# Four layers in one launch: other steps for two expert products of the last loop, and another order of tangents, weights and products

## What is computed

```python
# last attention: 16 heads of width 8, scores + a band mask, softmax, product with values, output matrix
x = x + L3_xattn(layernorm(x), ctx, ...)
# last feed-forward
y = layernorm(x)
logits = einsum('bsd,ed->bse', y, gate_w)               # 8 per token
topk_vals, topk_idx = top_k(logits, 2)
w = softmax(topk_vals)                                   # the two weights: (1 - t)/2, (1 + t)/2 with t = tanh(gap / 2)
full = scatter of w to 8 columns (six zeros)
expert_out = einsum('bsd,edh->bseh', y, weight)         # all eight experts
x = x + einsum('bse,bseh->bsh', full, expert_out)
```

## Time and profile before

| | |
|---|---|
| three runs | 846.9, 847.32, 849.75 us; median 847.32 us |
| profiled execution | 847.17 us |
| its span | 845.1 us (2.07 us lie around it) |
| last loop's steps 20 to 33, to the last store's issue | 805.4 to 841.5 us of the span |
| instructions | 20299 |

### The profile page before, as it was taken

One profiled execution on the slowest core, in us unless ns is written; L12 is line 12 of the kernel. 1 busy time (PEld: TensorE's weight loads), 2 busy tenths in 40 slices (PEclk: granted clock), 3 DMA queues, 4 the chain that ended last, 5 costly groups with the idle time before them and its releaser, 6 DMA issues.

```text
span 845.1 us, 20299 instructions
## 1 busy us (share of the span) xinstructions
PE 807.0 (95%) x7358; PEld 565.4 (67%) x7358; DVE 634.4 (75%) x1586; ACT 563.0 (67%) x1598; POOL 286.8 (34%) x587
## 2 busy tenths in 40 slices
PE   8999999999999999899999999999999989899986
PEld 8887888899998987554444444444466665676652
DVE  5678777777777665766966967756999967899876
ACT  3666667777767776686455666465577779888654
POOL 4246444455444335200000000002156630435445
PEclk9999999999999999999999999999999999999999
DMA  8700000000000000000000000000000000000000
GB/s 337 170 2 1 1 1 2 1 2 1 1 2 2 2 1 2 1 0 1 1 0 1 1 1 0 1 0 1 1 28 4 3 3 1 3 3 3 2 28 26
DMA packets 7886, 13.54 MB, mean 16 GB/s; under 512 B 4342, under 2 KB 5100, under 8 KB 7532
## 3 DMA queue, kind: packets, MB, share of 16 engines
q1 hardware_dynamic: 7788, 12.24, 4.6%
HBM read 11.19 MB, written 1.05 MB: 14 GB/s over the span
## 4 chain that ended last, share of the span: by engine, by line
PE 68%; DVE 14%; ACT 8%; issue 5%; POOL 4%; DMA 1%; DVEq 0%; POOLq 0%; SPq 0%; ACTq 0%
PE psum L1561 10%; PE psum L772 7%; PE psum L812 6%; PE psum L840 6%; PE psum L755 5%; PE psum L764 3%; ACT arena L910 2%; PE psum L1547 2%; PE psum L1570 2%; PE psum L2016 2%; PE psum L790 2%; PE psum L2401 2%; PE psum L829 2%; PE psum L2523 2%; PE psum L1986 2%
## 5 line engine op out<-in xcount | busy, mean ns | idle before, releaser
L517 POOL TENSOR_TENSOR ve<-mv,epsv 128x1 f32<-128x1 f32 x176 | 35.7, 203 | 422.0 <-DVE mv L512 422.0
L1561 PE MATMUL psum<-arena,w1f 128*128 128x512 f32 x240 | 109.5, 592 | 0.0
L520 POOL TENSOR_TENSOR rstd<-ve,epsv 128x1 f32<-128x1 f32 x176 | 101.3, 575 | 13.8
L910 ACT ACTIVATE arena<-psum,negmax 128x128 f32<-128x128 f32 x256 | 90.3, 405 | 22.2 <-DVE negmax L1010 22.2
L1561 PEld LDWEIGHTS psum<-arena,w1f 128*128 128x128 f32 x240 | 45.5, 190 | 48.6 <-issue 44.3
L1100 POOL TENSOR_TENSOR arena<-arena,rsum 128x512 f32<-128x512 f32 x64 | 65.7, 1046 | 24.6 <-DVE rsum L1016 24.6
L1010 DVE TENSOR_REDUCE negmax<-psum 128x8 f32<-128x1024 f32 x32 | 39.2, 1225 | 32.9 <-PE psum L812 32.9
L910 ACT ACTIVATION_READ_ACCUMULATOR arena<-psum,negmax 128x1 f32 x256 | 63.0, 246 | 0.0
L526 DVE TENSOR_SCALAR yln<-x_tok,mv,rstd 128x128 f32<-128x128 f32 x128 | 56.7, 454 | 7.9 <-POOL rstd L520 7.5
L755 PE MATMUL psum<-arena,sclA 128*128 128x128 f32 x512 | 62.5, 275 | 0.1
L772 PE MATMUL psum<-arena 128*128 128x512 f32 x128 | 61.5, 599 | 0.9 <-DVE arena L1005 0.6
(11 more groups left out here) (375 smaller groups left out, 1968.3 us busy)
## 6 DMA issues: line engine op xcount, KB each, us to landing
w<-in_w0qk SPq DMA_DIRECT2D x2, 512.0 KB, 4.9
w<-in_w0vo SPq DMA_DIRECT2D x1, 1024.0 KB, 7.6
cT<-in_cT SPq DMA_DIRECT2D x1, 1024.0 KB, 14.7
out<-x_tok SPq DMA_DIRECT2D x4, 256.0 KB, 2.2
rows<-in_rows SPq DMA_DIRECT2D x1, 836.0 KB, 12.3
x_tok<-in_x_tok SPq DMA_DIRECT2D x1, 768.0 KB, 9.7
ctx_tok<-in_ctx_tok SPq DMA_DIRECT2D x1, 768.0 KB, 10.9
wa<-in_wa SPq DMA_DIRECT2D x1, 768.0 KB, 16.8
```

The lines of the kernel that those rows point to most:

```text
L520: pool.tensor_tensor(rstd[:, u, self.i:self.i + 1], ve[:, u, self.i:self.i + 1], epsv[:, 1:2], ALU.pow) \
L910: m = nc.scalar.activation(e0[:, b, g, :], ps(k, P, j * P), ACT.Exp, bias=negmax0[:, b, g:g + 1], accum_out=sum0[:, b, g:g + 1])
L1561: nc.tensor.matmul(ps(k), w1("e2", j * 384 + arg * D, j * 384 + (arg + 1) * D), f1_Hm[:, n, 2 * j + i, :], start=False, stop=False)
```

## The change

It edits one table and two lists. Nothing else is touched, and no instruction is added or removed. Tile 6's products go from step 21 to step 20, tile 8's from step 23 to step 22. On ACT the tangent of a group stands ahead of the products of its step. On DVE the weights of a group stand ahead of the sums of its step, where they had stood at its end.

```diff
-        P_AT = (13, 14, 17, 18, 19, 20, 21, 21, 23, 23, 24, 25, 28, 31, 32, 33)
+        P_AT = (13, 14, 17, 18, 19, 20, 20, 21, 22, 23, 24, 25, 28, 31, 32, 33)
...
-        LATE_ACT = [("qk", 4), ("ot", 7), ("t", 6), ("v", 5), ("f3 p", 0), ("f2 round", 0), ("f2 store", 3), ("s", 5), ("f3 tanh", 0), ("lnt", 8)]
-        LATE_DVE = [("f3 top", 0), ("max", 5), ("f2 apply", 3), ("tail", 8), ("add", 7), ("s", 5), ("stats a", 7), ("f3 p", 0), ("f2 add", 2),
-                    ("rsum", 6), ("stats b", 7), ("f2 stats a", 2), ("av", 6), ("f2 stats b", 2), ("f2 whole", 0), ("f3 weights", 0)]
+        LATE_ACT = [("qk", 4), ("ot", 7), ("t", 6), ("v", 5), ("f3 tanh", 0), ("f3 p", 0), ("f2 round", 0), ("f2 store", 3), ("s", 5), ("lnt", 8)]
+        LATE_DVE = [("f3 top", 0), ("max", 5), ("f2 apply", 3), ("tail", 8), ("add", 7), ("s", 5), ("stats a", 7), ("f3 weights", 0), ("f3 p", 0), ("f2 add", 2),
+                    ("rsum", 6), ("stats b", 7), ("f2 stats a", 2), ("av", 6), ("f2 stats b", 2), ("f2 whole", 0)]
```

## The result

The kernel after takes 848.67 us (median of nine runs, 848.33 to 850.12), against 846.90 us for the kernel before in nine runs. The ratio is 1.0026 with a 95% interval of 1.0016 to 1.0037: about 2 us slower, less than 0.3% but beyond the interval. The forecast was 847.2 us and no change. In a second series the ratio was 1.0025 (1.0009 to 1.0041), median 849.32 us.

The account below looks back on a forecast made before the run. Bound: POOL's last tiles, fixed by when tile 11's sums end on VectorE. Terms -0.44 (tile 10's sums), +0.36 (step 25 weights), +0.10 (steps 12 and 17) sum to 0.0: 847.2 us, no change, range 845.5 to 848.9.

Parts of the forecast that it names:

- What bounds the kernel: Last loop's end: POOL at 1.75 us a tile, fixed by when tile 11's sums end on VectorE, behind tile 15's gate.
- No engine is full: Loop's end: claimed that no engine is fully busy there, so page totals do not price the change.
- Step 20: Tile 6's products ahead of `av` of tile 14: the group's copy comes at 813.33 us, 0.83 late.
- Step 21 gives it back, normalisation of tile 15 0.35 early: Sums of 1.04 and a wait of 0.54 us go, weights add 0.40: the 0.83 lateness becomes 0.35 early.
- Tile 8: Products in step 22: gate of tiles 12 to 14 later, but POOL less late, so tile 10's sums 0.44 us early.
- Weights in step 25: Weights now between group work and tile 11's sums: cost 0.36 us, bounds 0.3 to 0.7.
- Weights in step 21: Weights now ahead of tile 15's normalisation: add 0.40 us there.
- Steps 12 and 17: Weights ahead of normalisation, 0.4 us against 0.29 us of slack in step 17: 0.1 us late, bounds 0 to 0.4.
- The clock: Rival, chance 0.01: TensorE's 1.3 us wait before `ot` of tile 15 halves the clock, 14.2 us more, 861 us.
- TensorE's order takes what VectorE's gave: Rival, chance 0.11: step 20's late copy isn't made good in step 21, end 1.4 us late, 848.6 us.
- The upper end of the range: Whole kernel: 848.9 us, top of a range taking in both near rivals and the runs' scatter.

Follow-up runs that it names:

- e13: Kernel before with tile 6's products in step 20 and six useless matmuls ahead of the transpose of tile 13: 847.15 us.
- e2: Kernel before with only tile 8's products moved, to step 22: 845.85 us, ratio 0.999.
- e4: Kernel after with six useless matmuls on TensorE ahead of the transpose of tile 13: 847.22 us, ratio to before 1.0007.
- e9: e4 with the old order of tangents and weights, so only the two product steps are moved: 846.76 us.
- e7: e4 with tile 8's products back in step 23: 847.40 us.
- e8: e4 with tile 6's products back in step 21: 846.81 us.
- e5: e4 with POOL's two additions for tiles 5 and 6 cut to one column, their output left incomplete: 846.07 us.
- e3: Kernel after with the old product steps, so only tangents and weights stand in their new places: 847.33 us, ratio 1.0001.
- e11: Kernel before with the gate of tile 15 in step 28 instead of 25: 846.21 us, ratio 1.0001.
- e12: Kernel before with the gate of tile 15 in step 31 instead of 25: 845.15 us, ratio 0.9983; repeated, 845.72 us, ratio 0.9989.
- e1: Kernel before with only tile 6's products moved, to step 20: 846.73 us, ratio 0.9997.

## Why the prediction was wrong

| from L2110 of step 16 | us |
|---|---|
| before | 59.33 |
| tile 6's move (e13, 0.58 less 0.20 of added matmuls) | +0.38 |
| tile 8's move (e2) | +0.50 |
| order of tangents and weights (e4 less e9, 0.77 and the 0.20 of added matmuls in e9) | +0.97 |
| lower clock (after less e4) | +1.44 |
| sum | 62.62 |
| after | 62.66 |

The parts are not strictly additive: taken back out of the full change, tile 8's move is worth 0.21 us (e7) and tile 6's 0.94 (e8, with its added matmuls set apart), so the sum agrees better than its terms do. POOL's sums beside VectorE (e5) make 1.13 us, which lies across these rows and isn't one more. It is more than tile 6's whole move costs, since the early step by itself wins something: with the contention gone (e5) the normalisation of tile 15 comes 0.30 us sooner than with tile 6 back in step 21 (e8).

- **What bounds the kernel.** Right in the main. From the copy of tile 15's gate to the end it is 10.71 us before and 10.70 to 10.93 in the other traces with that gate in step 25, but for e3 and e7 (11.14 and 11.15). "No engine is full" was wrong: TensorE is busy 9.07 of 9.20 us from 830 on the earlier trace rows. And tile 11's sums have two things ahead of them that end together: in e9 VectorE waited 0.37 us behind the group work and started them 2.05 us behind TensorE's twenty passes, and before it is 2.05 us too (50.49 - 48.44). e11 and e12 move the gate on both engines and don't part the two.
- **Step 20.** Forecast: copy of the gate 0.83 late. From L2110 it is 31.97 against 30.62 us, 1.35 late, of which 0.45 comes from step 17. 0.90 is left (0.91 in e1, without the new order): right, though the 0.15 us for the release of the banks was an estimate without a row.
- **Step 21 gives it back, normalisation of tile 15 0.35 early.** This step failed. It was 38.08 - 36.71 = 1.37 late. Tile 6's sums and the 0.54 us wait did go, and the weights came to 0.52. But the group work took 3.40 us and not 2.26. With POOL's additions short (e5) the same normalisation is 0.15 late, 0.45 of lateness from step 17 included: 0.30 early without that, against the 0.35 forecast. So the terms of the sum were right, and the one that it lacks is VectorE beside POOL, 1.24 us at this place (38.10 in e4, 36.86 in e5). The prediction had the mechanism before it, in the row of 0.49 us, named the rule of the Trainium skill, "SBUF — State Buffer", section "SBUF: two separate sides", and applied it only to step 25. It didn't ask where POOL's own work goes when tile 6 moves. The two sums of POOL, 813.0 to 815.5, are laid over the group work exactly. By that rule each side blocks the other for a whole instruction; the ends of the stretched instructions, 0.02 to 0.04 us behind POOL's, agree with it. The prediction took the rule for instructions with two inputs; the conversion (L2572) has one and was stretched too.
- **Tile 8.** The forecast of the gate of step 23, later by the 1.77 us of the products, was right in size: 1.71 in e2. Expected was a net gain of 0.44 us at tile 10's sums. They did wait for products and no longer for POOL, as forecast (0.93 us in e2), but in e2 they start 47.52 us behind L2110, against 47.01: 0.51 late. Tile 10's products on TensorE came at 45.53 instead of 44.70. The prediction had them as before, 0.35 us of step 21 counted in; without that its own steps give 45.07. Most of the other 0.46 us is VectorE beside POOL's additions again, in step 23: the normalised row took 0.60 us and not 0.35, L2568 0.28 and not 0.16.
- **Weights in step 25.** Taken at 0.36. With the order alone changed it is 0.43 (e3), near the forecast. In the whole change it is 0.06 (10.77 us from the gate's copy to the end in e4, 10.71 before): with tile 8 written early, POOL starts tile 10's sum 0.34 us ahead of that copy and not 0.05, and stretches the group work less (L2568 0.16 us and not 0.29, L2572 0.20 and not 0.36), which takes 1.33 us to L2578 and not 1.63, and tile 11's sums have to wait for their products nearly as long in any case (2.12 us behind the first of the twenty passes in e4, 2.05 before).
- **Weights in step 21.** Taken at 0.40, inside the sum of step 21; measured 0.52 to 0.55. With tile 6 back in step 21 they cost nothing at the normalisation of tile 15 (e8: 0.45 late there, all of it from step 17), since they fit into the 0.54 us wait. It is tile 6's move, which removes that wait, that makes them cost.
- **Steps 12 and 17.** Taken at 0.1 in bounds of 0 to 0.4; measured 0.41, 0.45 at the gate. The argument that ScalarE hides it was wrong. The slack was taken too large as well: the normalisation of tile 11 ends 0.55 us later, and of the 0.29 us between its end and `ot` only 0.15 were slack, since 0.14 lie between them in the kernel after too.
- **The clock.** This rival had a chance of 0.01, with a price of 14.2 us. It came in both profiles of the kernel after, and cost 1.44 us in the first. Both numbers were wrong. The wait ahead of `ot` of tile 15 was foreseen (1.3 us, measured 1.45), the 0.72 us ahead of it was not. The chance was read off one row, the 1.61 us wait with the clock at 1.00 on both sides; in the 8 us ahead of that one TensorE had stood only 0.28 us, while here 0.72, 1.45 and 0.46 us of waits followed each other within 4.5 us. The price took all eight tiles at the lower clock, where the array was back at the higher one 3.4 us later; in e1, where it stayed low for some 10 us, the price was 4.1 us. "TensorE: Matmul & The Clock Gate" of the Trainium skill, section "What's actually happening", says that the clock depends on how busy the array has recently been. The trace agrees: TensorE was busy for 0.97 of 2.40 us and 1.12 of 1.60 us in the two stretches ahead of the fall.
- **The time.** "TensorE's order takes what VectorE's gave" had 848.6 us, and the median is 848.67. That agreement is luck: its condition, that tile 7's sums in step 21 still wait 0.54 us for products, did not come about. The upper end of the range, 848.9 us, is no better founded: the loop's end is 3.33 us longer in the trace, about twice what that end allowed.

The 1.8 and 2.7 us between the medians of the two series are less than the 3.33 us of the two traces. At equal clock it is 1.4 to 1.9 us, and before has falls of the clock of its own in some runs; how many of those are in this stretch isn't known, since only one run of a series leaves a trace.

## What to carry to other kernels

A moved step moves its work on every engine. For each move, lay the new times of all its instructions, POOL's too, over what VectorE does then; an addition of 0.7 us on POOL added 0.4 us to a VectorE instruction of 0.17. What an instruction costs also depends on the other moves: the weights of step 25 cost 0.43 us alone and 0.06 with tile 8 early. And price a wait on TensorE together with its neighbours: several short ones in a row brought the clock down where a longer one alone did not (though in e3 a fall stands behind a single one of 1.10 us, so the length of a wait doesn't settle it either way). A few matmuls without use in the gap took it back, for nothing where they end before the wait does (e4), for 0.2 us where they outlast it (e9, e13). Where a kernel's own clock scatters, compare times at equal clock or lengths in the trace from a common instruction, not medians alone, and follow a difference through several instructions of the chain before giving it to one step.

## What was not expected of the hardware

- The mean granted clock of one unchanged program on one core runs from 0.992 to 1.000, and its time with it by 6 us (0.7%). Seven of the seventeen traces here show a fall between 340 and 350 us, that of the kernel before behind a TensorE wait of 0.98 us, and others of the same code there show none, that of the kernel after behind one of 0.99 us.
- VectorE's conversion of 128x8 elements, with one input, was stretched from 0.17 to 0.63 us beside POOL, as were instructions with two inputs (0.17 to 0.59); the search for the places of the maxima (FIND_INDEX8, L2570), which ran beside POOL's addition too, kept its length (0.15 to 0.16 us each, before and after).
